# Expert layers of a hybrid network: token blocks of 128 rows for one expert become two half blocks of 64 rows on two 64-column tiles of the array

## What is computed

```python
top, at = two largest of (h @ Wg)
share = softmax(top)
y_e(h) = (silu(h @ W1[e]) * (h @ W3[e])) @ W2[e]
t = t + share[0] * y_at0(h) + share[1] * y_at1(h)
```

## Time and profile before

| | us |
|---|---|
| median of three runs | 1018.63 (1013.53 to 1019.27) |
| the profiled execution: its own time | 1018.52 |
| the profiled execution: its span | 1016.8 |
| last `turn_gated` minus first, layer 2 | 128.24 (22 intervals) |
| last `turn_gated` minus first, layer 3 | 257.09 (45 intervals) |

### The profile page before, as it was taken

How to read it: one execution, slowest core, us unless ns; L and a number is a source line. 1 busy time by engine, 2 the same in 40 slices (tenths; PEclk the granted TensorE clock), 3 DMA queues, 4 the chain that set the end, 5 groups by cost and what they waited for, 6 DMA issues and landing times. The chain is left out here.

```text
span 1016.8 us, 12888 instructions
## 1 busy us (share of the span) xinstructions
PE 837.7 (82%) x4088; PEld 538.6 (53%) x4089; DVE 452.6 (45%) x1165; ACT 301.3 (30%) x478; POOL 233.3 (23%) x314
## 2 busy tenths in 40 slices
PE   3769379899887986599999387876499999999993
PEld 2768237435743545366666344555356666666652
DVE  4974631698775645422222566645412121211213
ACT  3223235632244562012212144452021212222221
POOL 1150000573200100334433113340212211122110
PEclk8579677999898997699999597898699999999996
DMA  3000070000136503042111436832003007600003
GB/s 110 1 1 1 1 259 1 0 1 0 54 97 185 147 6 92 21 128 79 46 46 36 146 82 190 245 109 91 16 16 146 26 26 275 261 22 29 21 21 129
DMA packets 53621, 80.39 MB, mean 79 GB/s; under 512 B 10021, under 2 KB 45989, under 8 KB 50373
## 3 DMA queue, kind: packets, MB, share of 16 engines
q1 hardware_dynamic: 48040, 67.37, 20.5%
q0 software_dynamic: 5536, 12.46, 4.1%
HBM read 55.82 MB, written 11.27 MB: 66 GB/s over the span
## 5 line engine op out<-in xcount | busy, mean ns | idle before, releaser
L2096 PE MATMUL psum<-ring,f_x_t 128*128 x552 | 248.6, 593 | 1.3 <-DVE f_x_t L1961 1.3
L1954 DVE TENSOR_TENSOR f_gated<-f_silu,psum 128x512 f32<-128x512 f32 x69 | 47.5, 688 | 265.4 <-PE psum L2096 265.4
L2096 PEld LDWEIGHTS psum<-ring,f_x_t 128*128 128x128 f32 x552 | 99.5, 190 | 100.9 <-issue 100.8
L2110 PE MATMUL psum<-ring,f_gated_t 128*128 x552 | 130.7, 380 | 1.8 <-ACT f_gated_t L2020 1.8
L2110 PEld LDWEIGHTS psum<-ring,f_gated_t 128*128 128x128 f32 x552 | 101.2, 190 | 23.4 <-issue 12.7
L2020 ACT ACTIVATE f_gated_t<-psum 128x512 f32<-128x512 f32 x69 | 41.2, 597 | 235.0 <-PE psum L2103 231.5
L2016 ACT ACTIVATE f_silu<-psum 128x512 f32<-128x512 f32 x69 | 41.2, 597 | 116.5 <-PE psum L2096 109.8
L1114 PE MATMUL psum<-ident_sb 128*128 128x128 f32 x188 | 33.5, 347 | 30.8 <-PEq L2325 16.7
L1822 POOL COPY f_from_now<-f_from_row 128x1 uint32 (+1 forms) x48 | 9.0, 187 | 207.6 <-PE psum L2089 204.0
L1825 POOL DMA_INDIRECT f_xs<-rows_in,f_from_now x48 | 47.5, 989 | 36.5 <-POOL f_from_now L1822 36.5
L1834 POOL DMA_INDIRECT rows_out<-f_y,f_to_now x46 | 46.0, 1001 | 36.4 <-POOL f_to_now L1831 31.4
(11 more groups left out here) (295 smaller groups left out, 1259.1 us busy)
## 6 DMA issues: line engine op xcount, KB each, us to landing
ring<-in_f_experts SPq DMA_DIRECT2D x24, 1536.0 KB
a_stack_q<-a_parts SPq DMA_DIRECT2D x96, 64.0 KB, 2.0
a_stack_k<-a_parts SPq DMA_DIRECT2D x96, 64.0 KB, 2.0
rows_in<-h SPq DMA_DIRECT2D x4, 1024.0 KB, 5.8
ring<-rows_out SPq DMA_DIRECT2D x8, 512.0 KB, 5.8
a_wqkv<-in_a_wqkv SPq DMA_DIRECT2D x2, 768.0 KB, 4.4
x_in<-in_x SPq DMA_DIRECT2D x1, 1024.0 KB, 4.9
out<-x SPq DMA_DIRECT2D x4, 256.0 KB, 2.1
```

The source lines that it names most:

```text
L1954: dve.tensor_tensor(gated[:, b, :], silu[:, b, :], psum[:, 2 * b + 1, :], ALU.mult).then_inc(s_g, 1)
L2096: last = pe.matmul(psum[:, 2 * b + side, :], x_t[:, xb, t, :], k.ring[:, bass.ds(at + start, CHUNK)], start=(t == 0), stop=(t == CT - 1))
L2110: last = pe.matmul(psum[:, Y_BANK, 0:C], gated_t[:, b, P * a:P * a + P], k.ring[:, bass.ds(at + start, C)], start=(c == 0 and a == 0), sto ...
```

## The change

`HALF` = 64. Each expert's rows are now filled up to whole half blocks of 64, and a block of 128 rows is two half blocks that can belong to different experts. 2048 + 8 x 63 rows fit in 39 half blocks, so `MAXBLK` is 20: 20 chunk steps in layer 2, 40 in layer 3. The names:

- `up` and `down` issue each product twice, for rows 0 to 63 with weights from the ring and for rows 64 to 127 with weights from `w_up` or `w_down`; the first writes partitions 0 to 63 of the bank, the second 64 to 127. Each has 64 stationary columns.
- `w_up` and `w_down` are two buffers each on the chip for the second half's expert. ACT fills `w_up` from the ring (`copy_up`, two copies of 1024 columns for each chunk step), DVE fills `w_down` (`copy_down`, one of 1024). `s_wu` and `s_wd` count them, and TensorE waits for them. The wait for the load of a chunk moves from DVE's `take_x` to ACT's `copy_up`.
- `turn_x` moves from behind `up` to the place before it, next to `turn_gated`.
- The ring has 8 chunks: all eight experts of layer 2, four of layer 3. The scan loads 5, attention of layer 2 one, attention of layer 3 six, and the last two are issued at the start of the expert stage, ahead of the store of `rows_in`. In layer 3 each chunk is reloaded when `down` of that chunk is done (`s_dn[c]`), not when the whole block is.
- The space comes from tensors that are laid over the ring's last two chunks (`mixed`, `wqkv`, `rest`, `expo_low`). The last step of the loops is written out, and a silu of one column is put behind the router's exponential.

The core of the diff:

```diff
-MAXBLK = (2 * TOK + E * (P - 1)) // P
+HALF = P // 2
+MAXBLK = ((2 * TOK + E * (HALF - 1)) // HALF + 1) // 2
...
-RING_CHUNKS = 6
+RING_CHUNKS = 8
+SCAN_CHUNKS = 5
+ATTENTION_CHUNKS = 6
...
+            for n in range(ATTENTION_CHUNKS, RING_CHUNKS):
+                load_chunk(sp, k, w["experts"], chunks, n, s_loaded)
...
-                sp.wait_ge(s_loaded, 16 * chunks * e)
-                sp.wait_ge(s_y, done)
-                for n in range(chunks * e, chunks * e + chunks):
-                    load_chunk(sp, k, w["experts"], chunks, n, s_loaded)
+                for c in range(chunks):
+                    sp.wait_ge(s_loaded[c], 16 * e)
+                    sp.wait_ge(s_dn[c], done)
+                    load_chunk(sp, k, w["experts"], chunks, chunks * e + c, s_loaded)
...
             def take_x(j, b):
-                loads = dve.value_load(table[0:1, 1, bass.ds(j, 1)], min_val=16 * chunks, max_val=16 * chunks * E)
-                dve.wait_ge(s_loaded, loads)
                 dve.wait_ge(s_xt, j + 1)
...
+            def copy_down(j, c, b):
+                at = dve.value_load(table[0:1, 0, bass.ds(j, 1), 1:2], min_val=0, max_val=(RING_EXPERTS - 1) * chunks * CHUNK_COLS)
+                start = CHUNK_COLS * c + 2 * CT * CHUNK
+                used = j if chunks == 2 else j - 1
+                if above_zero(used):
+                    dve.wait_ge(s_dn[c], 2 * used)
+                dve.wait_ge(s_wu, 2 * (chunks * j + c) + 1)
+                dve.wait_ge(s_table, 1)
+                dve.tensor_copy(w_down[:, b, :], k.ring[:, bass.ds(at + start, CHUNK // P * C)]).then_inc(s_wd, 1)
...
+            def copy_up(second, c, side, b):
+                loads, at = second
+                start = CHUNK_COLS * c + CT * CHUNK * side
+                if side == 0:
+                    act.wait_ge(s_loaded[c], loads)
+                act.wait_ge(s_table, 1)
+                act.activation(w_up[:, b, CT * CHUNK * side:CT * CHUNK * (side + 1)],
+                               k.ring[:, bass.ds(at + start, CT * CHUNK)], ACT.Copy).then_inc(s_wu, 1)
...
             def up(q, xb, b, at, c):
                 for side in range(2):
+                    pe.wait_ge(s_wu, 2 * q + side + 1)
                     for t in range(CT):
-                        start = CHUNK_COLS * c + CHUNK * (CT * side + t)
-                        last = pe.matmul(psum[:, 2 * b + side, :], x_t[:, xb, t, :],
-                                         k.ring[:, bass.ds(at + start, CHUNK)], start=(t == 0), stop=(t == CT - 1))
+                        start = CHUNK * (CT * side + t)
+                        pe.matmul(psum[0:HALF, 2 * b + side, :], x_t[:, xb, t, 0:HALF],
+                                  k.ring[:, bass.ds(at + (CHUNK_COLS * c + start), CHUNK)], start=(t == 0), stop=(t == CT - 1))
+                        last = pe.matmul(psum[HALF:P, 2 * b + side, :], x_t[:, xb, t, HALF:P],
+                                         w_up[:, b, start:start + CHUNK], start=(t == 0), stop=(t == CT - 1))
                     last.then_inc(s_up, 1)
...
             def down(q, b, at, c):
                 pe.wait_ge(s_gto, q + 1)
+                pe.wait_ge(s_wd, q + 1)
...
+                    pe.matmul(psum[0:HALF, Y_BANK, 0:C], gated_t[:, b, P * a:P * a + HALF],
+                              k.ring[:, bass.ds(at + column, C)], start=start, stop=stop)
+                    last = pe.matmul(psum[HALF:P, Y_BANK, 0:C], gated_t[:, b, P * a + HALF:P * a + P],
+                                     w_down[:, b, C * a:C * a + C], start=start, stop=stop)
+                last.then_inc(s_dn[c], 2)
```

More of the change, by code:

```diff
@@ L1756, in experts_ffn @@
         s_xto = sm("x_t_out")
+        s_wu = sm("second_up_weights_copied")
+        s_wd = sm("second_down_weights_copied")
         s_up = sm("up_products")
@@ L1761, in experts_ffn @@
         s_gto = sm("gated_t_out")
[L1762 removed]
+        s_dn = [sm(f"down_products_{c}") for c in range(chunks)]
         s_y = sm("y_out")
@@ L1854, in _ @@
             turn(PAIRS - 1, more=False)
-            store_y(MAXBLK - 1, 0)
+            turn(PAIRS, more=False)
         @block.vector
@@ L2022, in _ @@
+            second = second_expert(0)
+            for side in range(2):
+                copy_up(second, 0, side, 0)
+            if chunks == 1:
+                second = second_expert(1)
+            copy_up(second, chunks - 1, 0, 1)
             silu_of(0, 0)
+            copy_up(second, chunks - 1, 1, 1)
             if chunks == 2:
                 take_gated(0, 0)
+                second = second_expert(1)
+                copy_up(second, 0, 0, 0)
                 silu_of(1, 1)
-            def turn(i):
-                for odd in (1, 0):
-                    j = 2 * i + (1 if odd else 2)
-                    for c in range(chunks):
-                        b = c if chunks == 2 else odd
-                        take_gated(chunks * j + c - 1, 1 - b)
-                        silu_of(chunks * j + c, b)
@@ L2035, in _, with block_step @@
-            turn(0)
+                copy_up(second, 0, 1, 0)
+            def block_step(i, odd, more=True):
+                j = 2 * i + (1 if odd else 2)
+                if chunks == 2:
+                    second = second_expert(j)
+                    take_gated(2 * j - 1, 1)
+                    copy_up(second, 1, 0, 1)
+                    silu_of(2 * j, 0)
+                    copy_up(second, 1, 1, 1)
+                    take_gated(2 * j, 0)
+                    if more:
+                        second = second_expert(j + 1)
+                        copy_up(second, 0, 0, 0)
+                    silu_of(2 * j + 1, 1)
+                    if more:
+                        copy_up(second, 0, 1, 0)
+                else:
+                    take_gated(j - 1, 1 - odd)
+                    if more:
+                        second = second_expert(j + 1)
+                        copy_up(second, 0, 0, 1 - odd)
+                    silu_of(j, odd)
+                    if more:
+                        copy_up(second, 0, 1, 1 - odd)
```

178 lines of the change are left out of this document (100 added, 78 removed).

## The result

The changed kernel takes 981.38 us (median of four runs, 979.93 to 982.63) where the kernel before takes 1016.91 in the same comparison: ratio 0.965, 95% interval 0.962 to 0.969. The profiled execution has a span of 979.4 us (before 1016.8) and a time of 981.07.

What follows compares the result with a forecast made beforehand. TensorE's stream was taken to bound both expert stages. Layer 2 -13.1, layer 3 -25.3, width changes at the loops' ends +0.6, loads and router -0.6: together -38.4 us from 1018.63, giving 980 us, range 970 to 1000.

Steps and rivals of the forecast that it cites:

- the side that had 90%: Whole kernel: faster by over 1%, chance 0.90; within 1% had 0.03, slower by over 1% had 0.07.
- Fewer steps: Both expert loops: 3 fewer intervals in layer 2, 6 in layer 3, at the old step price 51.7 us less.
- Two tiles side by side: `up` and `down` on TensorE: two 64-column tiles overlap fully, also at 512 columns, with nothing to pay for weight loads.
- Rival A: `up` and `down`: one weight load of 0.137 us exposed per pair, 132 us on top, 1112 us; 6% together with D.
- D: `down`: some 64-column product waits for a register, half the overlap gone, 0.87 us per chunk step, 1032; 6% with Rival A.
- Changing between widths: TensorE, each chunk step: two changes between 128 and 64 columns 0.18, second tile's lag 0.05, together 0.23 us (0.10 to 0.37).
- Copies of weights: ACT's and DVE's copies for the second half block: all hidden, 0; before the first block 0, up to +1 us.
- Rival B: Expert loops: ACT becomes the bound in layer 2, perhaps as much lost in layer 3, 1000 to 1020 us; 5%.
- Outside the loops: Stages around the loops: width changes at the ends +0.6 us, loads -0.3, router -0.3.
- Signs named beforehand: Trace: turns 6.05 and 5.94 us apart, `up` about 3.7, no waits on weight copies, clock 1.00, other stages within 3 us.
- C: Expert loops: width changes drain more or TensorE's queue runs short, 0.2 to 0.4 us more per chunk step, 992 to 1004; 7%.

## Why the prediction was right, and where its numbers were off

The forecast was 980.0 us, 981.4 was measured, inside the range, on the side that had 90%. Two misses of opposite sign stand behind the small difference: the loops gained 3.2 us less than forecast, the stages outside them 2.2 us more. That they nearly cancel is luck.

*Fewer steps.* Right to the hundredth: the price per step of the earlier trace rows times the steps, 51.7 us. The old loop with 21 blocks shows it without the rest of the change.

*Two tiles side by side.* Right: full overlap at 512 columns as at 256, and with the second tile removed, its loads with it, the loops are 0.4 us shorter out of 350. Rival A (weight loads exposed, 1112 us) and D fall with it: both tiles take in all rows, and their loads of 0.137 us cost nothing. The Trainium skill (TensorE: Matmul & The Clock Gate, section on packing small matmuls) says that a load of weights overlaps a running product only in another row group. The traces do not agree with that rule, and not only for column tiles: before the change loads of 0.190 us on the full array already ran beside passes 0.216 us apart. The loads of `down` (busy us, mean ns), before and after:

```profile
L2110 PEld LDWEIGHTS psum<-ring,f_gated_t 128*128 128x128 f32 x552 | 101.2, 190 | 23.4 <-issue 12.7
```

```profile
L2194 PEld LDWEIGHTS psum<-ring,f_gated_t 128*64 128x64 f32 x480 | 65.6, 137 | 61.2 <-issue 35.3
```

What the prediction did not see is a condition on the overlap, the order of the products: the earlier trace rows and the new loop both alternate, and with eight passes of one tile in a row the gain is gone (1034 and 1086 us).

*Changing between widths.* This term was mis-sized: "two changes 0.18, lag 0.05, together 0.23 us per chunk step" measured 0.30, inside the bounds of 0.10 to 0.37. The shorter overlap of two groups came as forecast: at the changes the next group starts 0.06 and 0.07 us before the last one's end (745.15 + 0.38 - 745.47; 745.96 + 0.38 - 746.27). The step that failed is taking that for the whole of a change. Each group after a change also has a longer first step, 0.05 to 0.06 us, which the last row already shows (0.44 for two transposes, 0.38 in the earlier trace rows) and I did not read; and the lag I had in its place is 0.007. The run with `turn_x` moved shows that the pair of changes carries all of it, the run with one tile that nothing else does. With no overlap at all at a change I had 988 us, 0.37 per step with my lag; the measured 0.30 lies between 0.23 and that. The Trainium skill (TensorEngine Tiling (Array Packing), key properties) says that changing the tiling mode drains TensorE. The trace agrees in that each change costs, and shows less than a full drain by its rows, whose ends are modelled.

The loops therefore came to -35.2 us, not -38.4: 58 intervals x 0.067 = 3.9 us less gain, 0.7 us given back at the ends, since the last step of each loop has no turn of tokens (0.22 and 0.11) and the extra 0.20 and 0.14 us of the old loops' intervals, which I had carried over, are gone.

*Copies of weights.* Right that they are hidden in the loops, 0 us, by doubling and by shortening them. At the start of layer 3 I had "0, up to +1"; it is 0.14, with no room left. The sizes: ACT 1.05 (I had 1.0), DVE 0.70 (I had 1.2, between 0.69 and 1.64); the copy has twice the columns of `gate` in the same time. Rival B was further off than I thought: ACT at 81% of the loops still costs nothing there.

*Outside the loops.* I had 0 in sum (+0.6 for changes, -0.3 attention, -0.3 router); it is -2.2 in the two profiled spans. The loads were undersized, -0.3 for what is 3.3 us in attention of layer 2: I took one wait of 1.04 us from the earlier trace rows, while the same stage has a second one of 3.5 us on the same transfers, and with three chunks TensorE waits there in two to four places (4.5 and 5.6 us in all) instead of one (2.6). Some of it may come back in the scan. The rest of the table is spread.

*Signs named beforehand.* Turns were to lie 6.05 and on average 5.94 apart: 6.12 and 6.01. `up` was to be a run of about 3.7 us, and from its first start to its last end it is (746.27 to 749.34 + 0.59). The stages outside the loops stayed inside 3 us. No wait on copies in the loops, and clock 1.00 there, came as said. Gaps at the groups' starts, the sign of C, came at a third of the size C has at least.

## What to carry over

When work fits 64 rows better than 128, two 64-column tiles give it at no price per pass, if the products of the two tiles stand next to each other in the program (up to four passes of one tile in a row still overlapped); what costs is every way out of the tile mode and back (0.30 us here), so put all full-width work in one place and multiply by the number of steps before counting the saving. A copy or a load that is asked for earlier also needs its source free earlier: look at who frees it before counting the gain. And work that is hidden in a loop can stand in the open before its first step: look there too.

## What the runs showed that I had not expected

- A pass of one tile starts ahead of passes of the other that stand before it in the program, as long as no more than three of them have yet to start, whatever their length (0.216 us in `down`, 0.429 in `up`). Each pass has its load of weights, so whether the reach counts passes or instructions is open. With alternate order the second tile lags 0.007 us, with twos of products 0.057.
- 4.7 us of idle TensorE was followed by 5 us at clock 0.51, which made a stall of 4.7 into one of 7.2.
- DVE's copy from SBUF to SBUF of 1024 float32 columns takes 0.70 us, as long as `gate`, its multiplication of 512 columns with an operand in PSUM, and stretches GpSimd's indirect gathers from 0.98 to 1.38 us. In layer 3 the scatters do not run beside it and keep their 1.01 us.
- Two loads of 1536 KB moved out of attention shorten that stage by 3.3 us, of which TensorE's waits on the stage's own transfers show 1.9 to 3.0.
